# Rope attention: values stored by partition, and loaded by indirect transfers from GpSimd's queue

## The reference, cut to what matters

```python
q = (src @ Wq).reshape(Bb, Tt, H, DH).transpose(0, 2, 1, 3)      # H = 16 heads, DH = 8
k = (src @ Wk_c @ Wk).reshape(Bb, Tt, H, DH).transpose(0, 2, 1, 3)
v = (src @ Wv_c @ Wv).reshape(Bb, Tt, H, DH).transpose(0, 2, 1, 3)
q, k = _apply_rope(q, sin, cos), _apply_rope(k, sin, cos)
attn = jax.nn.softmax(jnp.einsum('bhqd,bhkd->bhqk', q, k) / np.sqrt(DH), axis=-1)
sa = jnp.einsum('bhqk,bhkd->bhqd', attn, v)
```

## Time and profile before

| | us |
|---|---|
| median of 3 runs | 5035.45 (5034.88 to 5036.51) |
| the profiled execution's own time | 5037.02 |
| its span on the core | 5035.2 |
| TensorE busy | 4533.3 (90%) |
| VectorE busy | 3608.2 (72%) |
| ScalarE busy | 2332.0 (46%) |
| GpSimd busy | 812.9 (16%) |

### The profile page before, as it was taken

The page is one execution under the profiler, slowest core; times in us unless marked ns, Lnnn a source line. Parts: engine busy times, 40 slices in busy tenths (PEclk is TensorE's granted clock), DMA queues, the critical chain, the costliest instruction groups (busy, mean ns, idle before and its releaser), DMA issues. The chain is left out here.

```text
span 5035.2 us, 75510 instructions
## 1 busy us (share of the span) xinstructions
PE 4533.3 (90%) x25425; PEld 2134.6 (42%) x25425; DVE 3608.2 (72%) x8320; ACT 2332.0 (46%) x3145; POOL 812.9 (16%) x655
## 2 busy tenths in 40 slices
PE   4899999788999679999978989969999999998998
PEld 2222222443454312222244467744444444444776
DVE  6799999466666779999945677765656556556776
ACT  3477777422444337777742244433333333334443
POOL 3000000001000300000000000014444444443000
PEclk9799999799999879999988989979999999998999
DMA  3111111200000211111120010000000000001000
GB/s 94 37 41 43 41 42 41 94 0 30 1 0 0 59 49 39 45 38 45 39 78 23 0 38 1 1 21 2 2 2 2 2 2 2 2 2 39 1 0 17
DMA packets 233732, 127.60 MB, mean 25 GB/s; under 512 B 162152, under 2 KB 197916, under 8 KB 233308
## 3 DMA queue, kind: packets, MB, share of 16 engines
q1 hardware_dynamic: 225276, 106.04, 7.9%
q0 software_dynamic: 6432, 17.57, 1.4%
q10 hardware_dynamic: 1728, 0.28, 0.0%
HBM read 85.94 MB, written 36.70 MB: 24 GB/s over the span
## 5 line engine op out<-in xcount | busy, mean ns | idle before, releaser
L645 DVE TENSOR_REDUCE ra_mh<-PS 128x1 f32<-128x512 f32 x2144 | 1341.6, 681 | 153.3 <-PE PS L523 144.3
L600 ACT ACTIVATE ra_p<-PS 128x1024 f32<-128x1024 f32 x1040 | 1011.8, 1021 | 482.9 <-PE PS L530 474.6
L523 PE MATMUL PS<-ra_k,ra_q 96*128 96x512 bf16 x2144 | 749.8, 392 | 3.5 <-DVE ra_mh L645 3.2
L539 PE MATMUL PS<-ra_p,ra_va 128*32 128x512 f32 x4192 | 569.8, 608 | 70.5 <-ACT ra_va L593 70.3
L530 PE MATMUL PS<-ra_q,ra_k 99*128 99x512 bf16 x2080 | 622.5, 380 | 1.7
L1812 ACT ACTIVATE ca_p<-PS 128x1024 f32<-128x1024 f32 (+3 forms) x384 | 310.8, 809 | 589.2 <-PE PS L1742 384.6
L1881 DVE TENSOR_REDUCE ca_mh<-PS 128x1 f32<-128x512 f32 (+3 forms) x768 | 388.1, 551 | 153.1 <-PE PS L1702 123.8
L1441 ACT ACTIVATE f_hh<-PS,f_b 128x512 f32<-128x512 f32 x448 | 302.8, 687 | 390.4 <-PE PS L1397 390.1
L523 PEld LDWEIGHTS PS<-ra_k,ra_q 96*128 96x128 bf16 x2144 | 202.0, 97 | 660.9 <-DVE ra_mh L645 499.5
L1407 PEld LDWEIGHTS PS<-f_w,f_hh 128*128 128x128 f32 x3584 | 432.9, 192 | 99.5 <-issue 65.1
L1847 POOL TENSOR_TENSOR ca_s<-ca_s,ca_p 128x1024 f32<-128x1024 f32 (+3 forms) x256 | 414.0, 1617 | 234.8 <-ACT ca_p L1812 229.5
(11 more groups left out here) (242 smaller groups left out, 5481.2 us busy)
## 6 DMA issues: line engine op xcount, KB each, us to landing
ra_k<-qk_parts SPq DMA_DIRECT2D x136, 144.0 KB
ra_q<-qk_parts SPq DMA_DIRECT2D x408, 48.0 KB
o_heads<-ra_ot POOLq DMA_DIRECT2D x134, 128.0 KB, 2.9
ao_ot<-o_heads SPq DMA_DIRECT2D x16, 1024.0 KB, 6.4
qk_parts<-rp_parts SPq DMA_DIRECT2D x96, 128.0 KB, 2.3
ra_vc<-v_heads SPq DMA_DIRECT2D x34, 128.0 KB, 5.8
v_heads<-rp_vs SPq DMA_DIRECT2D x64, 64.0 KB, 1.9
ra_q<-ra_mp SPq DMA_DIRECT2D x198, 4.0 KB, 1.7
```

The source lines that it names most:

```text
L523: pe.matmul(PS[:, 5 + place % 3, :], Q[0:KMAX, u, j, t * P:(t + 1) * P], K[0:KMAX, u, j, h * BT:(h + 1) * BT], start=True, stop=True).then ...
L539: mm = pe.matmul(PS[VW * j:VW * (j + 1), 4, :], VA[:, ub, step % KT, j, :], PR[:, s % 2, j, :], start=(s % KT == 0) if start is None else ...
L600: act.activation(PR[:, s % 2, PH * pair:PH * (pair + 1), :], PS[:, PH * pair:PH * (pair + 1), :], ACT.Exp, scale=float(DH) ** -0.5).then_i ...
L645: dve.tensor_reduce(mh[:, pair, c // HALVES, c % HALVES:c % HALVES + 1], PS[:, bank, :], AX.X, ALU.max).then_inc(s_max, 1)
```

## The change

`v_heads` takes the layout [16 groups, 128 partitions, 8 tiles, 32 numbers], so that one partition's values of one group are one run of 1 KB; the four stores of a piece write runs of 512 bytes. The load of a group's values leaves SyncE's queue. GpSimd's queue issues it as an indirect transfer, which takes its 128 source rows from a tile of row numbers, `vr`. That tile is loaded from a new constant at the beginning of the attention block, and waited for. GpSimd then issues the first group's values, and, ahead of a group's stores, the next group's, behind a wait for ScalarE's copy of this group's.

```diff
-            V=nc.dram_tensor("v_heads", [BATCH * NG, SEQ, GH * DH], F32, kind="Internal").ap(),
+            V=nc.dram_tensor("v_heads", [BATCH * NG, P, KT, GH * DH], F32, kind="Internal").ap(),
...
-                            sp.dma_start(g["V"][NG * b + gi, u * BT:(u + 1) * BT, :].rearrange("(j p) c -> p j c", p=P),
+                            sp.dma_start(g["V"][NG * b + gi, :, u * TPB:(u + 1) * TPB, :],
                                          vs[:, u, :, gi * GH * DH:(gi + 1) * GH * DH]).then_inc(s_vst[u], 16)
...
+        vr = sb("ra_vr", [P, ITERS], mybir.dt.uint32)
+        s_vr = sem("ra_v_rows")
...
-                def values(n, u):
-                    sp.dma_start(vc[:, u, :, :], V[n].rearrange("(t p) c -> p t c", p=P)).then_inc(s_vl[u], 16)
-
...
                 load(0, 0, 0)
                 load(0, 1, 0)
-                values(0, 0)
                 max_rows(1, 0, 0)
...
                         load(after, 1, 1 - u)
-                        sp.wait_ge(s_va, n + 1)
-                        values(after, 1 - u)
                         max_rows(2 * n + 3, 0, 1 - u)
...
+                def values(n, u):
+
+                    pool.indirect_dma_start(vc[:, u, :, :].rearrange("p t c -> p (t c)"), None,
+                                            V.rearrange("n p t c -> (n p) (t c)"),
+                                            bass.IndirectOffsetOnAxis(vr[:, n:n + 1], 0)).then_inc(s_vl[u], 16)
+
+                pool.dma_start(vr[:, :], a["c_vrows"]).then_inc(s_vr, 16)
+                pool.wait_ge(s_vr, 16)
+                values(0, 0)
                 for n in range(ITERS):
+                    pool.wait_ge(s_va, n + 1)
+                    values((n + 1) % ITERS, (n + 1) % 2)
                     for h in range(2):
                         store(n, h)
...
+        "c_vrows": (P * np.arange(BATCH * NG)[None, :] + np.arange(P)[:, None]).astype(np.uint32),
```

More of the change, by code:

```diff
@@ L248, in rope @@
         rope_project(nc, a, g, buffers)
-        rope_attention(nc, g, buffers)
+        rope_attention(nc, a, g, buffers)
 def rope_project(nc, a, g, buffers):
@@ L398, in _, with rope_attention @@
                                 act.activation(parts[:, u, w, t, :], src[:, t, :], ACT.Copy).then_inc(s_h, 1)
-def rope_attention(nc, g, buffers):
+def rope_attention(nc, a, g, buffers):
     IDN, PS, QK, V, O = (g[k] for k in ("IDN", "PS", "QK", "V", "O"))
```

## The result

| | before | changed |
|---|---|---|
| median (20 runs each) | 5035.78 us | 5025.11 us |
| range of the runs | 5033.83 to 5038.5 | 5023.37 to 5029.45 |
| span of the profiled execution | 5035.2 | 5022.3 |

The ratio is 0.998, with a 95% interval of 0.9974 to 0.9987: 10.7 us less, where 20.9 were forecast. The way was right, the size half of what I said.

The account below looks back on a forecast made before the run. The prediction took TensorE's wait for the values at each attention call's start as the bound; gains of 10.6 and 10.3 us, all else zero, took the span from 5035.2 to 5014.3, median 5014.6 us, range 5010 to 5028.

Parts of the forecast that it names:

- What bounds the kernel: At each attention call's start, TensorE waits for ScalarE's copy of the values, 70.3 us in all; queries and keys come next.
- The first load: At the attention's start, GpSimd fetches row numbers in 2.9 us, then values in 4 us, landed at 130.3 us.
- the likeliest case: At the attention's start, queries and keys decide, first tile at 134.4 us; 5010.5 to 5019 us, chance 0.66.
- rival two: At the attention's start, GpSimd's chain decides, values landing after 132.1 us; 5019 to 5029 us, chance 0.20.
- The term of 20.9: Earlier first tiles at the start of both attention calls: 10.6 us gained in the first, 10.3 in the second.
- Rival three: At the attention's start, values stay hidden behind queries' and keys' data from whichever queue; 5029 to 5035 us, chance 0.09.
- "Nothing" for the 32 loads moved to GpSimd: In the steady groups, GpSimd's issue of the next values costs nothing, with 12.3 us until its next store.
- Rival four: In the steady groups, generating indirect transfers holds VectorE up, 32 times; 5077 us at 5 us a stall, chance 0.05.
- 3.7 us a stall: VectorE stall per steady group that eats up the 21 us gain, after 3.06 us of VectorE time left a group.
- The stores: In the projection, the values' stores with 512-byte runs change issue time by -2.8 to +2.8 us; taken as zero.
- The steady clock and the rest: After the first tile the chain shifts as a whole at VectorE's pace; TensorE's clock costs neither more nor less.
- the stated range: Forecast for the whole kernel's median time: 5010 us at the low end to 5028 us at the high end.

Follow-up runs that it names:

- Values first: The kernel before with one edit: SyncE issues the first group's values ahead of the queries and keys, layout and queue as before; 5017.85 us, ratio 0.9962.
- row numbers early: The changed kernel with the row numbers loaded already in the projection block, so the first indirect transfer is GpSimd's first attention work; 5023.94 us, ratio 0.9974.
- the other chip: The changed kernel itself, unedited, run again on another chip; 5028.6 us, against 5035.91 us for the kernel before there.
- the version with the stores: The kernel before with SyncE issuing the first values ahead of queries and keys, and the output stores moved from GpSimd's queue to SyncE's; 5004.32 us, ratio 0.9936.

## Why the prediction had the place right and the size wrong

Three steps of the sum failed: the landing of the two transfers at the start was put too low (20.9 us forecast from the first tiles, 18.0 measured), the 32 loads moved to GpSimd were put at nothing (they cost 4.4 us), and the drain at the block's end was left out (3.2 us).

**What bounds the kernel: right.** TensorE stood still for the values, and behind them lay the queries and keys. Values first shows it: first tile at 11.3 and 10.8 us, where I had worked out 11.0 from 0.58 MB and a landing.

**The first load: the likeliest case failed, rival two held.** I took 2.9 us for the row numbers and 4 us for the values, and found GpSimd's chain 1.8 us ahead of the queries and keys. It took 4.8 and 5.7 us in the first call, 3.3 and 5.4 in the second, and TensorE started the first tile directly behind the weighing matmuls in both. That is rival two, at a first tile of 13.4 us in the first call. In the second the two paths nearly tie: "row numbers early" has its first tile at 11.30 us there, held by the queries, against 11.48. The term of 20.9 measured 18.0 in the first trace and 16.9 in the one of the other chip. The median landing of the earlier trace rows was the wrong row: it was taken in groups where the DMA engines are mostly idle (a share of 0.14 in the earlier trace rows), and the first load runs beside queries and keys. The load of row numbers landed in 3.0 us there in the second call, and in 2.0 when "row numbers early" issued it in the projection block. The indirect transfer itself lands in 2.8 us at the median of its 34, and in 5.7 at its slowest; the slow ones are those of the start. One line's transfers in the changed kernel (ns, then landing):

```profile
L500 POOL DMA_INDIRECT ra_vc<-v_heads,ra_vr x34: 959/996/1051, 129.5 to 2494.9; - x34
...
DMA to landing us min/median/max: 2.7/2.8/5.7
```

Rival three, values hidden behind the data of queries and keys from whichever queue, would have put the first tile at 18.5 us after the first keys or later. It came at 13.4 and 11.5.

**"Nothing" for the 32 loads moved to GpSimd: wrong, 4.4 us.** I named 12.3 us of cover, the time to GpSimd's next store. That is the cover for an engine that waits for GpSimd. It isn't the cover for an instruction that GpSimd holds up while it issues. Rival four had the mechanism and the place, and drew its bound wrongly: I let VectorE's 3.06 us of idle time a group absorb a stall. But the casts stand in the turn, on which the ring of tiles waits, and 0.17 us there lengthened the group by 0.15. A stall is paid from the slack at its own place, and here there was next to none. The 3.7 us a stall at which I had the gain eaten up was therefore too high: with no slack, 20.9 / 32 = 0.65 us would have done it. The stall was 0.17, and that kept the sum positive.

**The end of the block: a term I did not have, 3.2 us.** I counted for a moved transfer its issue and its landing, and not the drain of the queue that it moves to. It was in the trace before: 5.54 us twice, which no busy share shows, since a drain isn't counted as busy. Its growth from 67 transfers to 85 is 1.47 us a block, and that is what the end grew by in the second call (1.47); in the first it grew by 1.78, and the 0.3 us more are open.

**The stores: zero was right.** 0.377 us each, and the layout alone changes nothing.

**The steady clock and the rest: right.** First exponentials follow the first tile by 30.7 us in both traces (from 144.98 to 175.71, and from 137.52 to 168.25); nothing of the shift is lost on the way, until the groups. TensorE's clock over that stretch was granted at 0.50 in the changed kernel's trace and at 0.56 before, and the 30.7 us are the same.

So 20.9 became 18.0 - 4.4 - 3.2 = 10.4. That the first median lies inside the stated range is luck: rival two alone, at its measured 18.0 us, gives 5017.5, and the 7.6 us that are missing then are two losses for which the sum had nothing. The second chip's 5028.6 lies above the range.

## What to carry to other kernels

When a transfer waits behind others in one queue, first try its place in that queue: here three lines in another order gave more than another layout, another engine and another form of transfer together. Before work is moved to GpSimd, price three things besides the issue: which VectorE instructions on the path it will run beside, how its landing looks beside the traffic of that moment, and the drain at the end of the block. And look at what all engines wait for between blocks; an engine off the critical path in every busy share can own that gap.

## What the runs showed of the hardware

- GpSimd's drain at the end of the attention block grew with the number of transfers that it had issued in it: 0.04 us with none, 5.54 with 67, 6.93 with 84, 7.01 with 85. That is 0.082 us for each (6.93 - 5.54 = 1.39 for 17). The 17 transfers more were plain in one kernel and indirect in another ("row numbers early"), and the drain was 6.93 us in both. It began some 2.5 us behind the last store's issue. The count is not all that can lengthen it: it was 3.70 us with 18 where it began with an indirect transfer under way, and in other blocks of this program, where GpSimd issues no transfer but computes, its drains take up to 1.2 us. SyncE, which issued 388 transfers in the same block and 67 stores more in the version with the stores, drained in 13 ns or less.
- An indirect transfer of 128 rows of 1 KB was issued in 1.00 us by GpSimd and landed 2.8 us after its issue began; the plain one of the same bytes 0.58 and 2.4 at the same place in the turn. Beside queries and keys on three engines, the first ones took 5.2 to 6.0 us until ScalarE's copy started where they were issued 3.8 to 5.5 us behind the first keys (indirect), and 4.4 and 4.7 (indirect) or 3.8 to 4.8 (plain) where they were issued within 0.8 us of them. Whether they waited there for what had been issued ahead of them or shared packet by packet, these traces don't settle.
- A cast of VectorE on 16 partitions was held from 0.21 to 0.38 us, up to the end of GpSimd's indirect issue. A plain issue in the same place held none of the 66; it ended before the cast that the indirect one had held began.
